# Gated cross-attention block: 128 instead of 256 moving columns in the second matmul of each score and PV product

## The chip, the cores and the metric

The kernel is written in Bass, with hand-placed semaphores, and runs on one core of one Trainium2 chip. A core has TensorE (matmul into PSUM), VectorE, ScalarE, GpSimd and SyncE, which here only issues DMAs. The metric is the device time of one execution in microseconds; the median of three executions is given, and one further execution was recorded by the profiler.

## The reference

A layer norm, cross-attention with 32 heads, a gated residual, a second layer norm, and a dense layer with LoRA adapters, for 32 batches of 64 tokens and 512 features:

```python
q = (hidden_q @ Wq).reshape(b, lq, h, dh)          # b=32, lq=64, h=32, dh=128
k = (hidden_kv @ Wk).reshape(b, lk, h, dh)
v = (hidden_kv @ Wv).reshape(b, lk, h, dh)
score = jnp.einsum('bqhd,bkhd->bhqk', q, k) * scale + position_bias
score = jnp.where(mask, score, neg_inf)
probs = jax.nn.softmax(score, axis=-1)
probs = jnp.where(mask, probs, 0)
ctx = jnp.einsum('bhqk,bkhd->bqhd', probs, v).reshape(b, lq, h * dh)
return ctx @ Wo
...
x = x + tanh(g_xattn[0]) * xattn(layernorm(x), ctx_4096, mask, position_bias, Wq, Wk, Wv, Wo)
x = x + tanh(g_ffn[0]) * ffn(layernorm(x), weight, bias, lora_A, lora_B, lora_start_indices)
```

The inputs are float32.

## The kernel before

**Precision.** Every matmul operand that matters is kept in two parts of type float32r (four bytes, of which TensorE uses a shortened mantissa): `hi` is the rounded value and `lo` the rest. A product of two such operands is made by `mm3` as three matmuls into the same PSUM bank: hi x hi, hi x lo, lo x hi, each with 512 moving columns in most places. The product lo x lo is left out there.

**Blocks and slots.** The 2048 rows are worked on in 4 blocks of 512 (8 batches). The main loop has one slot for each block and head, 128 in all, and each engine has its own instruction stream with a function `slot(n)`. TensorE's slot n is: the queries of head n (12 matmuls of `mm3`), the keys (12), one half of the value or output projection of a group of four heads (12), the two transposes of the probabilities of the slot before (line 437), the other half (12), then, in some slots, the transposes of the layer norm or the LoRA and dense work, then the scores of this slot and the PV product of the slot before. Order and waits are written out by hand; nothing schedules them.

**The score and PV block.** These two products are made differently. Four tiles m of 128 rows hold two batches each. For the scores, the stationary side is the queries of the tile, `qt_hi` or `qt_lo` (128 x 128), and the moving side is `kt[:, m, :, :, :]`, in which the hi part and the lo part of the keys lie side by side: 2 x 128 = 256 columns. `both` issues one matmul with the hi part of the stationary side and one with its lo part, both against all 256 columns, into `s_two[:, m, :, :]`, whose second index tells hi from lo of the moving side. So `s_two[:, m, 0, :]` holds (hi + lo) x hi, and `s_two[:, m, 1, :]` holds (hi + lo) x lo. VectorE adds the two halves as it scales them and adds the bias (line 746). The PV product is alike: stationary are the values `v` of tile t, hi or lo, moving is `pt[:, t, :, :]`, the transposed probabilities with hi and lo side by side, and the output is `pv_two[:, t, :, :]`, whose two halves are added by ScalarE and VectorE (lines 587 and 755). Each `both` has four tiles per product and slot, so a slot has 8 matmuls for the scores and 8 for PV.

**What waits for what around it.** The scores need `qt` and `kt` of this slot (written by ScalarE and VectorE). VectorE, GpSimd and ScalarE turn them into probabilities while TensorE makes the queries and keys of the next slot; GpSimd's scaling of `prob` (line 983) is what the transposes of line 437 wait for. ScalarE and VectorE copy the transposed probabilities into `pt` (lines 581 and 734), and PV waits for that. ScalarE takes PV's result out of PSUM (line 587).

In the names of the profile, `s_two<-kt,qt_lo` is a matmul into `s_two` with `kt` moving and `qt_lo` stationary; PE rows are matmuls and PEld rows are the loads of their stationary side, one for each.

Of the kernel before, what the change touches and what calls it, by code (L numbers as in the profile page):

```python
# [140 lines left out]
def flamingo_block(nc, x, ctxt, pair_bias, mask, wq, wk, wv, wo, g_xattn, g_ffn, wf, fbias, lora_a, lora_b,  # L141
                   lora_starts, lora_const, out):
    with ExitStack() as ctx:
# [131 lines left out]

        def both(pe, to, left, right):
            pe.matmul(to, left[0], right, start=True, stop=False)  # L277
            return pe.matmul(to, left[1], right, start=False, stop=True)  # L278

        block = ctx.enter_context(nc.Block())  # L280

# [92 lines left out]
        def _(pe):  # L374
# [65 lines left out]
            def scores(n):  # L440
                pe.wait_ge(q_lo, n + 1)
                pe.wait_ge(k_lo, n + 1)
                wait(pe, score_done, n)
                for m in range(PB):
                    mm = both(pe, s_two[:, m, :, :], [flat(q[:, m, :, :]) for q in qt], kt[:, m, :, :, :])
                mm.then_inc(s_ps, 1)

            def attention(n):
                g, h = divmod(n, G)
                pe.wait_ge(vo_free, NUMBER["v", g, PB - 1] + 1)  # L450
                pe.wait_ge(pt_lo, n + 1)
                for t in range(PB):
                    mm = both(pe, pv_two[:, t, :, :], parts(v, slice(None), h // 2 * (1 + g % 2), t, cols(h % 2, DH)), pt[:, t, :, :])
                mm.then_inc(pv_ps, 1)
# [608 lines left out]
```

## Time and profile before

| | us |
|---|---|
| median of 3 executions | 1824.71 (1824.16 to 1825.96) |
| the profiled execution | 1823.99 |
| span of its instructions | 1822.2 |
| matmuls | 8912, each with a weight load |
| of these on lines 277 and 278 | 4 x 512 |

The span is what the profile's views divide up; the execution's own time is 1.8 us longer. A busy time of TensorE is a sum of printed durations that overlap and whose ends are modelled; the distance from one start to the next is what a matmul takes from the engine in a dense run. Starts are printed in hundredths of a microsecond, so distances are read over several matmuls. The granted clock is 1.00 at full speed (2.4 GHz) and 0.5 at half (1.2 GHz).

### The profile page before, as it was taken

How to read it: one execution, taken by the hardware profiler on the slowest of the kernel's cores; microseconds unless marked ns; L12 is line 12 of the kernel's file. 1: busy time of each engine (PE TensorE's matmuls, PEld its weight loads, DVE VectorE, ACT ScalarE, POOL GpSimd, SP SyncE). 2: the span in 40 equal slices, each digit the busy share in tenths (PEclk: the TensorE clock that was granted, in tenths of full speed). 3: DMA queues.
4: the chain of work that ended last, by engine and by line, in shares of the span. 5: the costliest groups of instructions: out<-in, count | busy, mean ns of one | idle time of the engine just before them, and what ended most of it. 6: DMA issues, size and time to landing. Idle time of an engine off the chain costs nothing.

```text
span 1822.2 us, 25806 instructions
## 1 busy us (share of the span) xinstructions
PE 1774.6 (97%) x8912; PEld 1500.1 (82%) x8912; DVE 1165.9 (64%) x2257; ACT 808.7 (44%) x1608; POOL 923.0 (51%) x946
## 2 busy tenths in 40 slices
PE   5899999999999999999999999999999999999978
PEld 4788888888888888888888888888888888888866
DVE  4666667766677556766667656776667755666653
ACT  3444444444445434544445434444444543444430
POOL 3546455455555346554555534555555554545430
PEclk9999999999999999999999999999999999999987
DMA  3332333332332232323233223332323222232210
GB/s 119 93 114 82 104 99 110 99 94 86 98 100 87 93 110 92 112 81 105 81 104 93 88 93 110 98 105 91 95 83 101 90 82 98 81 99 83 91 35 24
DMA packets 93027, 168.76 MB, mean 93 GB/s; under 512 B 11313, under 2 KB 11441, under 8 KB 92898
## 3 DMA queue, kind: packets, MB, share of 16 engines
q1 hardware_dynamic: 91458, 165.52, 29.1%
q8 instruction: 72, 1.18, 0.3%
q10 hardware_dynamic: 1440, 1.59, 0.3%
q14 instruction: 57, 0.47, 0.1%
HBM read 162.88 MB, written 4.19 MB: 92 GB/s over the span
## 4 chain that ended last, share of the span: by engine, by line
PE 94%; DVE 3%; ACT 1%; issue 1%; DMA 0%; POOL 0%; SPq 0%; ACTq 0%; DVEq 0%
PE vo_bank L272 14%; PE vo_bank L274 14%; PE vo_bank L273 14%; PE q_bank L272 6%; PE q_bank L273 6%; PE q_bank L274 6%; PE k_bank L274 6%; PE k_bank L273 6%; PE k_bank L272 6%; PE pv_two L277 4%; PE pv_two L278 3%; PE s_two L278 3%; PE s_two L277 3%; PE pv_two L437 1%; PE vo_bank L461 1%; DVE wo_lo L689 1%
## 5 line engine op out<-in xcount | busy, mean ns | idle before, releaser
L973 POOL TENSOR_TENSOR score<-score,row_max 128x256 f32<-128x256 f32 x128 | 78.6, 614 | 679.3 <-DVE row_max L751 679.3
L929 POOL TENSOR_TENSOR ot_lo<-attn,ot_hi 128x512 fp32r<-128x512 f32 x128 | 165.6, 1294 | 112.9 <-ACT ot_hi L527 112.9
L272 PE MATMUL vo_bank<-wv_hi,ct_hi 128*128 128x512 f32 x512 | 205.6, 401 | 15.3 <-POOL wv_lo L929 15.3
L587 ACT ACTIVATE attn<-pv_two 128x512 f32<-128x512 f32 x128 | 76.7, 599 | 315.8 <-PE pv_two L278 315.8
L272 PE MATMUL vo_bank<-wo_hi,ot_hi 128*128 128x512 f32 x512 | 206.2, 403 | 3.5 <-POOL ot_lo L929 3.5
L272 PE MATMUL q_bank<-xt_hi,wq_hi 128*128 128x512 f32 x512 | 202.3, 395 | 1.4 <-DVE xt_lo L689 1.4
L273 PE MATMUL q_bank<-xt_lo,wq_hi 128*128 128x512 f32 x512 | 201.7, 394 | 0.0
L274 PE MATMUL vo_bank<-wo_hi,ot_lo 128*128 128x512 f32 x512 | 201.3, 393 | 0.0
L274 PE MATMUL vo_bank<-wv_hi,ct_lo 128*128 128x512 f32 x512 | 201.0, 392 | 0.0
L273 PE MATMUL vo_bank<-wo_lo,ot_hi 128*128 128x512 f32 x512 | 200.8, 392 | 0.0
L273 PE MATMUL vo_bank<-wv_lo,ct_hi 128*128 128x512 f32 x512 | 200.5, 392 | 0.0
L274 PE MATMUL q_bank<-xt_hi,wq_lo 128*128 128x512 f32 x512 | 200.2, 391 | 0.0
L274 PE MATMUL k_bank<-ct_hi,wk_lo 128*128 128x512 f32 x512 | 199.2, 389 | 0.0
L273 PE MATMUL k_bank<-ct_lo,wk_hi 128*128 128x512 f32 x512 | 199.2, 389 | 0.0
L272 PE MATMUL k_bank<-ct_hi,wk_hi 128*128 128x512 f32 x512 | 199.2, 389 | 0.0
L689 DVE TENSOR_TENSOR kt<-k_bank,kt 128x512 fp32r<-128x512 f32 x128 | 88.7, 693 | 146.5 <-ACT kt L527 146.5
L527 ACT ACTIVATE ot_hi<-attn 128x512 fp32r<-128x512 f32 x128 | 81.2, 634 | 219.2 <-DVE attn L755 219.2
L719 DVE TENSOR_TENSOR acc<-vo_bank,acc 128x512 f32<-128x512 f32 x128 | 88.4, 690 | 140.6 <-PE vo_bank L274 140.6
L929 POOL TENSOR_TENSOR wq_lo<-raw_q,wq_hi 128x512 fp32r<-128x512 f32 x128 | 166.2, 1299 | 21.7 <-ACT wq_hi L527 21.7
L929 POOL TENSOR_TENSOR wk_lo<-raw_k,wk_hi 128x512 fp32r<-128x512 f32 x128 | 175.1, 1368 | 2.1 <-ACT wk_hi L527 2.1
L929 POOL TENSOR_TENSOR wv_lo<-raw_vo,wv_hi 128x512 fp32r<-128x512 f32 x124 | 157.6, 1293 | 0.0
L689 DVE TENSOR_TENSOR wo_lo<-raw_vo,wo_hi 128x512 fp32r<-128x512 f32 x128 | 143.7, 1161 | 21.6 <-ACT wo_hi L527 21.5
(107 smaller groups left out, 4186.3 us busy)
## 6 DMA issues: line engine op xcount, KB each, us to landing
raw_vo<-in_wo SPq DMA_DIRECT2D x128, 256.0 KB, 3.3
raw_q<-in_wq SPq DMA_DIRECT2D x127, 256.0 KB, 2.6
raw_k<-in_wk SPq DMA_DIRECT2D x127, 256.0 KB, 2.8
raw_vo<-in_wv SPq DMA_DIRECT2D x124, 256.0 KB, 3.5
raw_bias<-in_pair_bias SPq DMA_DIRECT2D x64, 256.0 KB, 3.2
acc<-in_x SPq DMA_DIRECT2D x16, 256.0 KB, 5.4
out<-acc SPq DMA_DIRECT2D x16, 256.0 KB, 2.0
stage<-in_ctxt SPq DMA_DIRECT2D x14, 256.0 KB, 2.8
```

Of the source, the lines that this page charges most:

```text
L272: pe.matmul(to, left[0], right[0], start=first, stop=False)
L273: pe.matmul(to, left[0], right[1], start=False, stop=False)
L274: return pe.matmul(to, left[1], right[0], start=False, stop=last)
L277: pe.matmul(to, left[0], right, start=True, stop=False)
L278: return pe.matmul(to, left[1], right, start=False, stop=True)
L437: mm = pe.transpose(t_bank[:, cols(j, P)], flat(prob[:, cols(j, 2), :]), ident[:, :])
L527: act.activation(to, src, func).then_inc(done, 1)
L587: act.activation(by(attn, PB), pv_two[:, :, 1, :], ACT.Copy).then_inc(ot_b, 1)
L689: dve.tensor_tensor(to, src, f32(of), ALU.subtract).then_inc(done, 1)
L719: dve.tensor_tensor(acc[b % 2][:, t, :], bank_of(job)[:, :], acc[b % 2][:, t, :], ALU.add).then_inc(vo_free, 1)
L929: pool.tensor_tensor(to, src, f32(of), ALU.subtract).then_inc(done, 1)
L973: pool.tensor_tensor(score[:, :, :], score[:, :, :], row_max[:, :].unsqueeze(2).to_broadcast([P, PB, S]), ALU.subtract).then_inc(shift_don ...
```

## The change

```diff
         def both(pe, to, left, right):
             pe.matmul(to, left[0], right, start=True, stop=False)
-            return pe.matmul(to, left[1], right, start=False, stop=True)
+            return pe.matmul(to[:, 0, :], left[1], right[:, 0], start=False, stop=True)
```

`right` is `kt[:, m]` or `pt[:, t]`, whose second index is the part. With the change, the lo part of the stationary side meets only the 128 columns with the hi part of the moving side, and its matmul adds only to the first half of the output. The second half then holds hi x lo alone, and lo x lo is computed nowhere, as with `mm3`. The number, the order, the weight loads, the waits and the semaphore increments of TensorE's instructions stay as they are, and the instructions of all other engines and the DMAs are the same.

## Rows read from the trace of the kernel before

**Rows 1.** The page: busy time by engine, and the chain by engine.
```profile
PE 1774.6 (97%) x8912; PEld 1500.1 (82%) x8912; DVE 1165.9 (64%) x2257; ACT 808.7 (44%) x1608; POOL 923.0 (51%) x946
...
PE 94%; DVE 3%; ACT 1%; issue 1%; DMA 0%; POOL 0%; SPq 0%; ACTq 0%; DVEq 0%
```

**Rows 2.** Busy time from 60 to 1760 us; TensorE's waits there (total, times, longest).
```profile
core 0: us, PE busy (x) PEld busy (x) DVE busy (x) ACT busy (x) POOL busy (x), PEclk, DMA share, GB/s
60.00:1760.00 1700.00, 1695.76 (x8591) 1436.78 (x8591) 1113.10 (x2147) 779.22 (x1553) 893.47 (x907) 1.00 0.30 94
...
PE pv_two L277 <- DVE pt L734: 2.0, 4, 1.2
PE s_two L277 <- issue: 1.3, 1, 1.3
```

**Rows 3.** TensorE's waits over the whole run: total us, times, longest us.
```profile
PE vo_bank L272 <- POOL wv_lo L929: 15.3, 1, 15.3
...
PE pv_two L277 <- DVE pt L734: 5.1, 7, 1.9
```

**Rows 4.** TensorE's matmuls in order of time: start us, duration us, engine, line.
```profile
702.96 0.39 PE L272 MATMUL vo_bank<-wo_hi,ot_hi 128*128 128x512 f32 x1
...
703.64 0.28 PE L277 MATMUL s_two<-kt,qt_hi 128*128 128x256 f32 x1
703.76 0.28 PE L278 MATMUL s_two<-kt,qt_lo 128*128 128x256 f32 x1
...
704.60 0.28 PE L277 MATMUL pv_two<-pt,v_hi 128*128 128x256 f32 x1
...
705.44 0.28 PE L278 MATMUL pv_two<-pt,v_lo 128*128 128x256 f32 x1
705.56 0.40 PE L272 MATMUL q_bank<-xt_hi,wq_hi 128*128 128x512 f32 x1
```

**Rows 5.** Line 278 over the whole run: count, duration ns min/median/max.
```profile
L278 PE MATMUL s_two<-kt,qt_lo x512: 278/283/415, 42.7 to 1763.2; 128*128 128x256 f32 x171
...
L278 PE MATMUL pv_two<-pt,v_lo x512: 278/283/415, 56.1 to 1774.2; 128*128 128x256 f32 x171
```

**Rows 6.** TensorE's weight loads in the same score block, in order of time.
```profile
703.65 0.19 PEld L278 LDWEIGHTS s_two<-kt,qt_lo 128*128 128x128 f32 x1
703.76 0.19 PEld L277 LDWEIGHTS s_two<-kt,qt_hi 128*128 128x128 f32 x1
```

**Rows 7.** Weight loads at two places where TensorE had been idle.
```profile
65.98 0.19 PEld L277 LDWEIGHTS s_two<-kt,qt_hi 128*128 128x128 f32 x1 [1.51 <-issue]
66.09 0.19 PEld L278 LDWEIGHTS s_two<-kt,qt_lo 128*128 128x128 f32 x1
...
502.29 0.19 PEld L277 LDWEIGHTS pv_two<-pt,v_hi 128*128 128x128 f32 x1 [0.30 <-issue]
502.40 0.19 PEld L278 LDWEIGHTS pv_two<-pt,v_lo 128*128 128x128 f32 x1
```

**Rows 8.** Transposes (128 moving columns): eight in a row, durations, loads behind two.
```profile
30.87 1.03 PE L461 MATMUL vo_bank<-ident,xn 128*128 128x128 f32 x8
...
L461 PE MATMUL vo_bank<-ident,xn x128: 271/273/476, 30.9 to 1799.5; 128*128 128x128 f32 x128
...
700.79 0.19 PEld L272 LDWEIGHTS vo_bank<-wo_hi,ot_hi 128*128 128x128 f32 x1
700.89 0.19 PEld L273 LDWEIGHTS vo_bank<-wo_lo,ot_hi 128*128 128x128 f32 x1
```

**Rows 9.** Matmuls of the PV block at half clock, in order of time.
```profile
56.11 0.41 PE L278 MATMUL pv_two<-pt,v_lo 128*128 128x256 f32 x1
56.32 0.41 PE L277 MATMUL pv_two<-pt,v_hi 128*128 128x256 f32 x1
```

**Rows 10.** What other engines deliver to TensorE around the block, in order of time.
```profile
701.96 0.86 DVE L734 TENSOR_TENSOR pt<-pv_two,pt 64x256 fp32r<-64x256 f32 x2 [0.37 <-ACT pt L581]
...
710.02 0.62 POOL L983 TENSOR_TENSOR prob<-prob,row_scale 128x256 f32<-128x256 f32 x1
...
713.75 0.38 PE L437 MATMUL pv_two<-ident,prob 128*128 128x128 f32 x2
```

## The prediction

> **What bounds the kernel now.** I read the page first, from its busy shares to its chain. TensorE is busy for 97% of the span, and 94% of the chain that ended last is its own work; the next engine on the chain is VectorE with 3% [rows 1]. A busy share alone proves little for TensorE, whose matmul ends are modelled, so I asked for two more views. The table of stretches shows 1695.8 us of matmul in the 1700 us from 60 to 1760 at a granted clock of 1.00, and the list of waits of the same stretch has three entries, 3.8 us together (2.0, 1.3 and one of 0.5) [rows 2]. So between those points TensorE runs one matmul behind the other, and what one matmul costs is the distance from its start to the next start, not its printed duration: the 256-column matmuls have a duration of 283 ns but start every 120 ns. Outside that stretch TensorE waits more, 15.3 us for the first weights alone [rows 3], at the start and at the tail, which the change hardly touches.
>
> The starts give the price list. In the score and PV block of one slot sixteen 256-column matmuls start from 703.64 to 705.44, and the next one, of 512 columns, starts at 705.56: 1.92 us / 16 = 120 ns each. From the 512-column matmul at 702.96 to the first 256-column one at 703.64 lie three of 512 columns, 227 ns each [rows 4]. The difference of 256 columns is 107 ns, which is 256 / 2.4 GHz, and what is left over is 227 - 2 x 107 = 13 ns (120 - 107 = 13 ns too) for each matmul whatever its width. The granted clock is full there, so this is the upper level, 2.4 GHz.
>
> **The change, part by part.** It adds and removes no instruction and moves none: every `both` still issues two matmuls, each with its weight load, in the same order and with the same semaphores. The first (L277) is as it was. The second (L278) streams 128 columns in place of 256. There are 512 of these for the scores and 512 for PV [rows 5]; four of the first and eight of the second kind fall in the two short stretches of half clock, at the start and in the tail, so that 1012 run at full clock.
>
> By columns alone, the second matmul should go from 120 ns to 13 + 128 / 2.4 = 67 ns. [...] The views of the weight loads tell when the load runs: in this block the load of the next matmul starts 2 to 3 ns behind the start of the current one (load at 703.65 behind the matmul of 703.64, load at 703.76 with the matmul of 703.76) [rows 4, 6], so only one load is ahead, and the distance between two starts can't be shorter than one load. What a load takes is hidden in a block where starts are 120 ns apart. It shows where TensorE restarts from idle: there the first weights go in with nothing in flight, and the second load begins once the first is done. 65.98 to 66.09 and 502.29 to 502.40: 110 ns each as printed in hundredths [rows 7]; the printed duration of 0.19 us has a latency in it that overlaps. A sharper value comes from the four transposes of line 461 or the two of line 437, which have 128 moving columns: eight of them take 1.03 us in all, the last one 0.273 us of it, so they start every (1.03 - 0.273) / 7 = 108 ns. And behind two of them, the load for the 512-column matmul begins at 700.79 and the one after it at 700.89: 100 to 110 ns for one load of the float32r kind, beside a 128-column transpose [rows 8].
>
> So I take 108 ns for the distance from a 128-column second matmul to the next start: one load. The load for the second matmul itself is covered by the 256 columns of the first, as now. Per pair that is 120 + 108 = 228 ns in place of 240. The sum: 1012 x (120 - 108) = 12.1 us.
>
> At half clock the 256-column matmuls start every 210 ns [rows 9], which is 256 / 1.2 GHz, the lower level. If a load keeps its 108 ns there, the twelve matmuls win 12 x 0.1 = 1.2 us; if it is clocked like the columns it takes 216 ns and they win nothing. I take nothing, as no row shows a load at half clock that is shorter than 200 ns.
>
> Both bounds of the unknown: no row shows a float32r matmul with 128 moving columns. Upper end of the gain by the nearest rows: 108 ns for the second matmul, and the first one perhaps 113 ns in place of 120, as the first pair of the score block (703.64 to 703.76) is a little shorter than the others, if a stream that has ended early lets the pair close up; that is 760 x 7 ns = 5.3 us more, 17.4 us in all. Lower end: the second matmul at 120 ns still, no gain; at 113 ns, as that first pair, 7.1 us. I take the 108, because it is the only distance that rows show behind a matmul with 128 moving columns.
>
> What is late next? The score block ends 4 x 12 = 48 ns sooner and the PV block 96 ns sooner in each slot of some 13 us, and everything behind it comes forward with it. Two results of other engines have to be there. The transposed probabilities: VectorE has written them at 701.96 + 0.86 = 702.82, and the first PV matmul starts at 704.60 [rows 4], 1.8 us later. The scaled probabilities: GpSimd is done at 710.02 + 0.62 = 710.64, the transposes start at 713.75 [rows 10]. 48 ns doesn't use up such slack. Where TensorE waits for the transposed probabilities already (7 times in the run, 4 of them between 60 and 1760 [rows 2, 3]), the shorter score block ahead only lengthens the wait: 7 x 48 ns = 0.3 us given back. Net 12.1 - 0.3 = 11.8 us.
>
> Against the profiled execution: span 1822.2 - 11.8 = 1810.4 us, execution 1824.0 - 11.8 = 1812.2 us. Its time lies 0.7 us under the median of 1824.7, so the median forecast is 1824.7 - 11.8 = **1812.9 us**, 0.65% less.
>
> [...]
>
> **The rivals.**
>
> *No change.* The 13 ns above 107 belong to the exchange of weights and not to the stream, so that a start that waits for a load costs 107 + 13 = 120 ns again. For it: a load and 256 columns take the same 107 ns, so the block of before can't tell which of them carries the 13. Against it: the 108 ns behind the transposes and at the restarts [rows 7, 8]. It gives 1824.7 us. Chance 0.12.
>
> *The whole columns are won.* If the weights could go in two ahead, the second matmul would cost 67 ns and the gain is 1012 x 53 = 53.6 us, 1771 us. Against it: each load starts just behind the start of the matmul before it [rows 6]. [...] Chance 0.04.
>
> *Slower: narrow moving data run in several passes.* The transposes show that 128 columns of four-byte data can cost more than the line through 256 and 512 says: 108 ns where it says 67, about two times 53 ns [rows 8]. If a 128-column float32r matmul takes four times its columns, it costs 4 x 53 + 13 = 227 ns in place of 120, and the kernel loses 1012 x 107 = 108 us: 1933 us. Two passes would be hidden by the load; it decides from where the distance is over 120 ns. Against it: the transposes are plain float32, a transpose is another mode, and at 256 columns nothing of the kind shows. [...] Chance 0.11.
>
> *Slower: the clock.* The arrays stream fewer columns in the same blocks. A stretch of half clock of some 17 us, as in the tail, doubles what TensorE does in it and costs 8.5 us; two of them in mid-run turn the gain into a loss (1821 us with one, 1830 with two). Against it: the clock stays full from 60 to 1760 [rows 2], across blocks in which TensorE pauses for 1.2 and 1.3 us. Chance 0.03.
>
> **How the numbers follow.** The forecast has a chance of 0.70 and its own range is 1806.5 (both matmuls closer) to 1818 (113 ns). The range to hold 8 in 10 adds the case of no change (0.12) and so goes from 1806.5 to 1826, 1.3 us above the median for the scatter of the runs; it leaves out 0.18. A measurement of this kernel can tell about 0.2%, 3.6 us, from no change. Faster: 0.70 + 0.04 = 0.74. Same: 0.12. Slower: 0.11 + 0.03 = 0.14.
>
> **What would show it.** In the profile of the changed kernel the score and PV block should be 16 matmuls in about 8 x 0.228 = 1.82 us, with starts alternating between 120 and 108 ns; and the load that follows a second matmul should start with it. If the first is right and the span falls by less, waits of TensorE between 60 and 1760 should have grown beyond 4 us. Starts evenly 120 ns apart mean that the 13 ns is the exchange. A distance of over 200 ns behind L278 means passes. If the load of the next weights starts ahead of the current matmul, my one-load floor is wrong. If the time differs and the block doesn't, the prediction is wrong in a way that I don't see.

## The result and the profile after

The changed kernel takes 1819.8 us in the median of 15 executions (1816.9 to 1822.4), the kernel before 1824.3 us in 15 beside them (1822.6 to 1826.7). The ratio is 0.9975, 95% interval 0.9967 to 0.9982: faster by 0.25% or 4.5 us. The forecast was 11.8 us. The direction was right, but the gain is only 38% of the one forecast. The time lies inside the stated range of 1806.5 to 1826 only because that range was widened for the case of no change; it lies outside the forecast's own range, which ended at 1818.

The two profiled spans differ by just 1.7 us (1822.2 and 1820.5), so a difference of spans says little about where the gain went. What helps is that the program is periodic. From the first keys matmul (line 272) of slot 4 to the last line-272 one of slot 127 both kernels run the same order of instructions: 123 slots and nine more keys matmuls (2.0 us in each kernel). The rows below are the view of one tile, `k_bank`, from slot 4 on: engine and operation, count, duration in ns (min/median/max), first and last start in us. First the kernel before:

```profile
L272 PE MATMUL k_bank<-ct_hi,wk_hi x496: 389/389/389, 85.3 to 1760.0; 128*128 128x512 f32 x166
```

and the changed kernel:

```profile
L272 PE MATMUL k_bank<-ct_hi,wk_hi x496: 389/389/389, 89.2 to 1757.7; 128*128 128x512 f32 x166
```

This stretch took 1674.7 us before and 1668.5 us after: 6.2 us won, 50 ns a slot where 96 were forecast. And the changed kernel comes to slot 4 already 3.9 us late. These are two separate shortfalls. A third, small one is behind the last of these rows: 62.2 us to the end of the span before, 62.8 us after. Together: 6.2 - 3.9 - 0.6 = 1.7 us.

**The start.** The table of stretches shows a difference there. The columns are the stretch and its length, the busy time of each engine, the granted clock, the DMA share and GB/s. The kernel before and the changed one from 43.5 to 76.5 us:

```profile
43.50:76.50 33.00, 26.58 (x117) 21.64 (x117) 19.65 (x50) 13.55 (x28) 21.01 (x23) 0.90 0.31 95
```

```profile
43.50:76.50 33.00, 27.26 (x106) 22.06 (x107) 19.19 (x48) 11.30 (x25) 20.42 (x21) 0.74 0.34 95
```

The mean clock is 0.74 in place of 0.90, and TensorE gets 106 matmuls started where it had started 117. One more thing differs, and earlier. TensorE starts at 15.2 to 15.3 us in both, and its first matmuls of 512 columns stand 427 ns apart, at half clock. The first one that is shorter than 0.6 us, before and after:

```profile
19.25 0.42 PE L272 MATMUL vo_bank<-wv_hi,ct_hi 128*128 128x512 f32 x1
```

```profile
20.86 0.46 PE L273 MATMUL vo_bank<-wv_lo,ct_hi 128*128 128x512 f32 x1
```

Full clock comes 1.6 to 1.7 us later in this execution of the changed kernel, ahead of any matmul that the change touches. So not all of the 3.9 us need come from the change.

**The block.** TensorE's matmuls in order of time in the changed kernel, around a score and PV block (start us, duration us):

```profile
705.15 0.39 PE L274 MATMUL vo_bank<-wo_hi,ot_lo 128*128 128x512 f32 x1
705.38 0.28 PE L277 MATMUL s_two<-kt,qt_hi 128*128 128x256 f32 x1
705.49 0.22 PE L278 MATMUL s_two<-kt,qt_lo 128*128 128x128 f32 x1
705.55 0.34 PE L277 MATMUL s_two<-kt,qt_hi 128*128 128x256 f32 x1
705.72 0.22 PE L278 MATMUL s_two<-kt,qt_lo 128*128 128x128 f32 x1
...
707.11 0.22 PE L278 MATMUL pv_two<-pt,v_lo 128*128 128x128 f32 x1
707.17 0.45 PE L272 MATMUL q_bank<-xt_hi,wq_hi 128*128 128x512 f32 x1
707.45 0.39 PE L273 MATMUL q_bank<-xt_lo,wq_hi 128*128 128x512 f32 x1
```

These answer to [rows 4]. A first matmul (L277) now has a printed start only 60 ns behind that of the narrow one ahead of it, and a duration of 0.34 us in place of 0.28; from it to the next start it is 170 ns (705.55 to 705.72). Printed starts of matmuls don't come at an even pace here. Those of the weight loads come every 110 to 130 ns, so I read the distances from them, in the same block:

```profile
705.49 0.19 PEld L277 LDWEIGHTS s_two<-kt,qt_hi 128*128 128x128 f32 x1
705.60 0.19 PEld L278 LDWEIGHTS s_two<-kt,qt_lo 128*128 128x128 f32 x1
705.72 0.19 PEld L277 LDWEIGHTS s_two<-kt,qt_hi 128*128 128x128 f32 x1
...
706.88 0.19 PEld L277 LDWEIGHTS pv_two<-pt,v_hi 128*128 128x128 f32 x1
706.99 0.19 PEld L278 LDWEIGHTS pv_two<-pt,v_lo 128*128 128x128 f32 x1
707.11 0.19 PEld L272 LDWEIGHTS q_bank<-xt_hi,wq_hi 128*128 128x128 f32 x1
```

Before, two such loads stood 110 to 120 ns apart [rows 6]. Now they alternate: 110 ns as printed from the load behind a narrow matmul to the next, and 120 to 130 ns from there; in the trace's nanoseconds, as medians over many slots, 108 to 110 and 120 to 126 ns. From 705.49 to 707.11 lie seven pairs in 1.62 us, 231 ns a pair; before it was 240, and the forecast had 228. So the principle of the forecast (one load behind a narrow matmul, one 256-column stream behind a wide one) comes within 3 ns of each pair.

Then something is given back behind the block. From the first score matmul to the second matmul of the next queries it was 703.64 to 705.79 before and is 705.38 to 707.45 now. The printed hundredths give 2.15 and 2.07 us; the nanoseconds of the trace give 2.146 and 2.078 us, 68 ns ahead (73 ns at the third matmul of the queries). To the first keys matmul, eleven 512-column matmuls on, it was 4.66 us (708.30) and is 4.60 us. The row of the changed kernel:

```profile
709.98 0.39 PE L272 MATMUL k_bank<-ct_hi,wk_hi 128*128 128x512 f32 x1
```

60 ns are left. The 512-column matmuls behind the block don't start every 227 ns at once: before, the first five distances are mostly 228 to 236 ns, and in the changed kernel this lasts two matmuls longer.

I call the 75 of the 123 slots that take 13.07 us before plain slots; they have no layer norm, LoRA or dense work in them. Their median is the same 68 ns ahead behind the block, and 60 ns kept. The other 48 slots keep 39 ns in the mean, which brings the mean slot to 50 ns. TensorE waits a little more: the lists of waits from 90 to 1755 us have 1.3 us before and 2.3 us after. Before:

```profile
PE pv_two L277 <- DVE pt L734: 0.8, 3, 0.3
PE vo_bank L461 <- DVE v_lo L689: 0.5, 3, 0.2
```

After:

```profile
PE pv_two L277 <- DVE pt L734: 1.6, 6, 0.3
PE vo_bank L461 <- DVE v_lo L689: 0.7, 3, 0.2
```

### The profile page after: what moved, and what is told of

Same layout as the page of the kernel before. It is cut to its first block, busy times and chain, and to the rows that moved or that the text cites. A ratio compares the mean times of both kernels' runs of the same rounds, so it can differ in the third digit from the quotient of the medians.

```text
span 1820.5 us, 25806 instructions
## 1 busy us (share of the span) xinstructions
PE 1773.2 (97%) x8912; PEld 1495.9 (82%) x8912; DVE 1168.6 (64%) x2257; ACT 807.0 (44%) x1608; POOL 922.8 (51%) x946
## 4 chain that ended last, share of the span: by engine, by line
PE 93%; DVE 3%; ACT 1%; issue 1%; DMA 0%; POOL 0%; SPq 0%; ACTq 0%; DVEq 0%
PE vo_bank L272 13%; PE vo_bank L274 13%; PE vo_bank L273 13%; PE q_bank L272 7%; PE q_bank L274 6%; PE q_bank L273 6%; PE k_bank L274 6%; PE k_bank L272 6%; PE k_bank L273 6%; PE pv_two L277 5%; PE s_two L277 4%; PE pv_two L278 2%; PE s_two L278 2%; PE pv_two L437 1%; DVE wo_lo L689 1%
## 5 line engine op out<-in xcount | busy, mean ns | idle before, releaser
L272 PE MATMUL vo_bank<-wv_hi,ct_hi 128*128 128x512 f32 x512 | 205.9, 402 | 15.2 <-POOL wv_lo L929 15.2
L272 PE MATMUL q_bank<-xt_hi,wq_hi 128*128 128x512 f32 x512 | 211.2, 413 | 1.4 <-DVE xt_lo L689 1.4
L587 ACT ACTIVATE attn<-pv_two 128x512 f32<-128x512 f32 x128 | 76.5, 598 | 303.1 <-PE pv_two L278 303.1
```

What stands on the lines that cost most here:

```text
L272: pe.matmul(to, left[0], right[0], start=first, stop=False)
L587: act.activation(by(attn, PB), pv_two[:, :, 1, :], ACT.Copy).then_inc(ot_b, 1)
```

## Experiments

### The start: narrow late, narrow early, narrow from slot 2

The edit against the changed kernel, shortened:

```diff
-        def both(pe, to, left, right):
+        def both(pe, to, left, right, narrow):
             pe.matmul(to, left[0], right, start=True, stop=False)
-            return pe.matmul(to[:, 0, :], left[1], right[:, 0], start=False, stop=True)
+            if narrow:
+                return pe.matmul(to[:, 0, :], left[1], right[:, 0], start=False, stop=True)
+            return pe.matmul(to, left[1], right, start=False, stop=True)
...
+                    mm = both(..., n >= 4)      # late;  early: n < 4;  from slot 2: n >= 2
```

Expected of the late change:

> The second matmul is narrow (128 columns) from slot 4 on; in slots 0 to 3 it has 256 columns as before. In the profile of the changed kernel TensorE lost some 3.9 us on the kernel before by the third slot, most of it in added stretches of half clock between 45 and 76 us, and won 6.2 us from there to slot 127, 50 to 60 ns a slot. Theory A (the narrow matmuls of the first slots bring the half clock about): this kernel has the early slots of the kernel before and all of the later gain, so 1824.3 - 6 = 1818 us in every run, mean clock 0.989 or 0.990, runs within 1.5 us of each other. Theory B (the stretches come and go whatever the width): the runs scatter over 1817 to 1822 us as those of the changed kernel did, with clocks from 0.986 to 0.990, and those of the kernel before scatter by the same.

Measured: 1817.8 us (1816.2 to 1819.2, 5 executions), ratio 0.9963, interval 0.9950 to 0.9975. Clocks 0.989 or 0.990 in all five. The same row of `k_bank`:

```profile
L272 PE MATMUL k_bank<-ct_hi,wk_hi x496: 389/389/389, 85.0 to 1753.4; 128*128 128x512 f32 x166
```

1668.4 us for the stretch of 123 slots, as with the full change (1668.5), and slot 4 begins at 85.0, not 89.2. The clocks are those of theory A; the times lie 3 us apart, not within the 1.5 us that it expected. The clock from 43.5 to 76.5 us is that of before:

```profile
43.50:76.50 33.00, 26.83 (x123) 21.98 (x123) 20.15 (x50) 13.82 (x29) 21.76 (x23) 0.90 0.32 95
```

> Narrow second matmul in slots 0 to 3 only; everything from slot 4 on as before. Theory A (the width of the first slots brings the half clock): slower than the kernel before by about 4 us in most runs, mean clock about 0.986. Theory B: the same as the kernel before within 0.5 us in the median (4 slots x 60 ns = 0.2 us won), the scatter of both alike.

Measured: 1825.6 us (1823.3 to 1826.8, 11 executions), ratio 1.0005, interval 0.9996 to 1.0014: no difference that can be told. Theory A had about 4 us more. But the executions fall into two sorts: 7 of 11 have a mean clock of 0.987 or 0.988, with 1825.5 us or more, and 4 have 0.990, with 1823.3 to 1825.0. Of the 35 executions of the kernel before that stand beside these experiments, one is below 0.989. The profiled one is of the first sort:

```profile
L272 PE MATMUL k_bank<-ct_hi,wk_hi x496: 389/389/389, 89.1 to 1763.8; 128*128 128x512 f32 x166
```

It is 3.8 us late at slot 4 and still 3.8 us late at slot 127; the slots between take 1674.7 us, as before. Behind them it takes 60.5 us to the end, 1.7 us less than the kernel before. So the tail varies too, and a mean clock covers the start and the tail: it doesn't tell by itself where the half clock was.

> Narrow second matmul from slot 2 on, slots 0 and 1 wide. In the changed kernel's profile the first added stretch of half clock (some 2.4 us lost) lies about slot 1 and the second (2.7 us) at 69 to 76 us, slots 2 and 3. If the narrow blocks of slots 2 and 3 alone are enough, about half of the runs show a mean clock of 0.988 or less and take 1820 to 1822 us; if it takes the narrow blocks of slots 0 and 1, all runs are at 0.989 or 0.990 and 1816 to 1819 us.

Measured: 1817.0 us (1816.1 to 1822.4, 5 executions), ratio 0.9966, interval 0.9954 to 0.9979. One of the five has 0.987 and 1822.4 us, the other four have 0.989 or 0.990 and at most 1817.5 us. One in five is neither of the two outcomes that were expected (about half, or none).

What follows: neither theory as it was written. The 15 executions of the changed kernel are of two sorts too: 9 with a clock of 0.986 to 0.988 and 1819.5 to 1822.4 us, 6 with 0.989 or 0.990 and 1816.9 to 1818.0 us. With narrow matmuls in all of slots 0 to 3, 16 of 26 timed executions (changed kernel and early) have a mean clock below 0.989, against 1 of 35 of the kernel before. With slots 0 to 3 wide it is none of the 5 late ones and, in the runs further below, 1 of 6 and 0 of 5, and one profile (the last matmul wide) had the added half clock. So narrow first slots make it likely and don't force it, and wide ones don't quite exclude it. An execution with the lower clock takes 4.4 us longer in the changed kernel (medians 1821.9 and 1817.5 us) and 2.1 us longer in the early one (1826.1 and 1824.0).

A rival to the width of the first slots is left: the moment at which full clock first comes. In the three profiles with added half clock from 43.5 to 76.5 us (changed, early, and the last matmul wide) it first came at 21.0 to 21.3 us, in nine without it at 18.2 to 19.7. But in the two with 192 and 64 columns it came at 21.1 us as well, and no half clock was added; they came to slot 4 at 86.6 and 86.7 us, against 84.8 to 85.6 us for the nine. So a late first rise goes with some 1 to 1.5 of the 3.9 us by itself, and every added half clock that was profiled came with one. Whether it takes both, no run shows; what in the first blocks tips the clock wasn't isolated.

### Which half wins what

Same edit, `narrow` true for the scores alone or for PV alone, in all slots. Each of these two, and of the next three kernels, ran once.

> Narrow second matmul in the scores, 256 columns in PV as before. Of the gain per slot, 8 pairs x 12 ns = 96 ns forecast and 50 to 60 ns seen. Theory C (every 256-column matmul behind a narrow one starts its successor 2 to 4 ns later than before, and the first 512-column matmul of the queries 7 ns later): the scores win 4 x 9 = 36 ns a slot, none lost at the queries, since a wide matmul is last: 30 to 36 ns a slot. Theory D (a fixed price of some 40 ns a slot, paid elsewhere): 4 x 12 - 40 = about 8 ns a slot.

> Narrow second matmul in PV, 256 columns in the scores as before. Theory C: 4 x 9 = 36 ns won less 7 ns at the first 512-column matmul of the queries behind it: 22 to 30 ns a slot. Theory D: about 8 ns a slot, and the two halves together win more than their sum.

Measured, the `k_bank` rows of the scores alone and of PV alone:

```profile
L272 PE MATMUL k_bank<-ct_hi,wk_hi x496: 389/389/389, 85.0 to 1755.7; 128*128 128x512 f32 x166
```

```profile
L272 PE MATMUL k_bank<-ct_hi,wk_hi x496: 389/389/389, 85.6 to 1757.4; 128*128 128x512 f32 x166
```

1670.7 and 1671.8 us (the executions took 1820.4 and 1821.1 us): 33 and 24 ns a slot. Theory C has both, theory D (8 ns each) falls. In the mean slot the two sum to 57 ns, against 50 together; in the plain slots they keep 33 and 27 ns, which is the 60 of the change. In the scores alone, where the PV block behind is wide, the 33 ns won are all kept; PV alone is 35 ns ahead behind the block and keeps 27.

### Does the load bind: 192, 64, and 128 on both sides

From slot 4 on, the second matmul with 192 or 64 columns; and both matmuls with 128. With 64 columns half of lo x hi is left out, and with both at 128 all of hi x lo, so these two only serve to measure time. The edits against the changed kernel, shortened:

```diff
-                return pe.matmul(to[:, 0, :], left[1], right[:, 0], start=False, stop=True)
+                return pe.matmul(to[first 192 or 64 columns], left[1], right[the same], start=False, stop=True)
...
-            pe.matmul(to, left[0], right, start=True, stop=False)
+            pe.matmul(to[:, 0, :], left[0], right[:, 0], start=True, stop=False)     # both at 128
```

> From slot 4 on the second matmul has 192 moving columns, between the 128 of the change and the 256 of before (half of lo x lo is computed). Slots 0 to 3 as before, as in the kernel with the late change. Theory E (the distance to the next start is the longer of one weight load, 108 to 109 ns, and 13 ns + columns / 2.4): 13 + 80 = 93 ns is under the load, so 192 columns cost what 128 do, and a slot wins the same 50 to 60 ns. Theory F (cost falls with the columns, in proportion): half the gain, 25 to 30 ns a slot.

> From slot 4 on the second matmul has 64 moving columns; half of lo x hi is left out of the scores and of PV. Slots 0 to 3 as before. Theory E: the load of 108 to 109 ns binds as with 128 columns, 50 to 60 ns won a slot, nothing more. Theory F: 75 to 90 ns a slot.

> From slot 4 on the first matmul has 128 moving columns too; hi x lo is left out of the scores and of PV. Every distance of the block is then one load. Theory E: 16 x 109 = 1.74 us for the block in place of the 1.92 us of before and some 1.85 us of the change; per slot 16 x 11 = 176 ns won less 7 ns at the queries, 165 to 175 ns. If the loads themselves grow when they follow each other without a break (a load is 108 ns only when the array is otherwise idle for half the time), the distance is 115 to 120 ns and the gain 60 to 80 ns.

Measured, in this order:

```profile
L272 PE MATMUL k_bank<-ct_hi,wk_hi x496: 389/389/389, 86.6 to 1755.0; 128*128 128x512 f32 x166
```

```profile
L272 PE MATMUL k_bank<-ct_hi,wk_hi x496: 389/389/389, 86.7 to 1752.6; 128*128 128x512 f32 x166
```

```profile
L272 PE MATMUL k_bank<-ct_hi,wk_hi x496: 389/389/389, 85.5 to 1749.6; 128*128 128x512 f32 x166
```

192 columns: 1668.4 us (the execution took 1819.0 us), 51 ns a slot, just what 128 give. Theory E has it and theory F (half the gain) falls: between 128 and 192 columns the width of the second matmul is worth nothing. The distance behind the narrow matmul, read from the loads, is 108 to 110 ns with 192 columns as with 128, where 13 ns + columns / 2.4 gives 93 and 67 ns.

64 columns: 1665.9 us (the execution took 1815.6 us), 72 ns a slot, 80 in the plain slots. Theory E said 50 to 60; F said 75 to 90, but its proportion to the columns is out by the 192. The load behind the narrow matmul still takes its 108 to 110 ns; what shrank is the other distance of the pair, which its loads show:

```profile
701.97 0.19 PEld L277 LDWEIGHTS s_two<-kt,qt_hi 128*128 128x128 f32 x1
702.08 0.19 PEld L279 LDWEIGHTS s_two<-kt,qt_lo 128*128 128x128 f32 x1
702.19 0.19 PEld L277 LDWEIGHTS s_two<-kt,qt_hi 128*128 128x128 f32 x1
...
702.88 0.19 PEld L277 LDWEIGHTS pv_two<-pt,v_hi 128*128 128x128 f32 x1
```

Four pairs in 0.91 us are 228 ns each, which is the pair that was forecast for 128 columns. With half the columns again the 3 ns are gone. The block is 100 ns ahead at the second matmul of the queries, and 20 ns of that are given back. Why a wide matmul is slowed by 3 ns more behind 128 or 192 columns than behind 64 isn't explained by a floor of one load.

Both at 128: 1664.1 us (the execution took 1814.1 us), 86 ns a slot, where E said 165 to 175 and its alternative 60 to 80. The loads in the block:

```profile
700.03 0.19 PEld L282 LDWEIGHTS s_two<-kt,qt_lo 128*128 128x128 f32 x1
700.14 0.19 PEld L278 LDWEIGHTS s_two<-kt,qt_hi 128*128 128x128 f32 x1
700.25 0.19 PEld L282 LDWEIGHTS s_two<-kt,qt_lo 128*128 128x128 f32 x1
...
701.70 0.19 PEld L272 LDWEIGHTS q_bank<-xt_hi,wq_hi 128*128 128x128 f32 x1
701.81 0.19 PEld L273 LDWEIGHTS q_bank<-xt_lo,wq_hi 128*128 128x128 f32 x1
702.06 0.19 PEld L274 LDWEIGHTS q_bank<-xt_hi,wq_lo 128*128 128x128 f32 x1
```

From 700.03 to 701.70 lie 15 distances, 111 ns each. That is the cost of a float32r matmul of 128 columns whose neighbours are no wider. It is 3 ns over the 108 that the forecast took for a load, and 3 ns is also what a load's start lies behind the start of the matmul beside it. At the load for the third matmul of the queries (702.06, which goes with the start of their second) the block stands at 2.03 us against 2.15 before, 120 ns ahead; 93 ns are kept in the plain slots. The give-back is 27 ns here, 8 ns in the changed kernel counted from the same matmul (13 from its peak).

### The order: two wide, two narrow

From slot 4 on, with nothing left out that the change computes. The two tiles of a pair, m and m + 2, lie 512 float32 columns apart in PSUM. The edit for the scores, shortened; PV has the same:

```diff
+                    for m in range(2):
+                        for j in (m, m + 2):
+                            pe.matmul(s_two[:, j, :, :], hi of tile j, kt[:, j, :, :, :], start=True, stop=False)
+                        for j in (m, m + 2):
+                            mm = pe.matmul(s_two[:, j, 0, :], lo of tile j, kt[:, j, 0, :, :], start=False, stop=True)
```

> From slot 4 on the same matmuls as in the change, in another order: two first (256 columns) of two tiles that lie in different PSUM banks, then their two second ones (128 columns). Nothing is left out that the change computes. Theory G (a matmul of 256 or 512 columns that starts right behind its own load, with no earlier stream still running, takes some 3 to 7 ns more): it is now 4 of the 8 first matmuls in place of 8 that start so, and the slot wins 3 x 4 = 12 ns more than the late change does, 62 to 75 ns in the plain slots in place of 60. Rival: the 3 ns belong to every 256-column matmul whose next one is narrow or to the load of the second part; then the order changes nothing.

> The paired order again, timed. In the look at it its plain slots were 66 ns shorter than before (late change: 60), and it gave 1817.5 us against 1824.5. Theory A again (narrow matmuls in slots 0 to 3 bring the half clock there): wide in those slots, it should show mean clocks of 0.989 or 0.990 in every run, as the late change did. Forecast: 1817 us, 0.7 us under the late change, which its scatter of 3 us may hide.

Measured: 1817.9 us (1816.2 to 1819.0, 6 executions), ratio 0.9965, interval 0.9953 to 0.9977; an execution ahead of these, profiled too, took 1817.5 us. The slots:

```profile
L272 PE MATMUL k_bank<-ct_hi,wk_hi x496: 389/389/389, 85.6 to 1753.4; 128*128 128x512 f32 x166
```

1667.8 us, 56 ns a slot against 51 of the late change (1667.7 us in the other profile). The plain slots keep 7 ns more, 67 in place of 60; theory G expected 2 to 15 more and its rival nothing. But the 7 ns are not where theory G put them. From the first score matmul to the second matmul of the queries:

```profile
701.48 0.40 PE L452 MATMUL s_two<-kt,qt_hi 128*128 128x256 f32 x2
...
703.56 0.40 PE L273 MATMUL q_bank<-xt_lo,wq_hi 128*128 128x512 f32 x1
```

That is 2.08 us, and 2.08 us in the late change (701.12 to 703.20). The order wins nothing in the block (67 and 68 ns ahead in the plain slots); what differs is that the queries behind it give nothing back. So theory G isn't borne out, though its number came true. In time the kernel can't be told from the late change. All clocks were 0.989 but one, of 0.988. Counted as above, that one is low; its time, 1816.2 us, is the shortest of the six, and no profile tells where its half clock lay.

### The last matmul wide

As the late change, with `n >= 4 and t < 3` for PV, so that tile 3 has its 256 columns back. It ran once.

> As the late change, but the last tile of PV has its second matmul wide (256 columns): 7 narrow ones a slot. Seen so far: with all 8 narrow, the block is 68 to 73 ns ahead of before at the second 512-column matmul of the queries behind it, and 12 to 13 ns of that are given back over the next six; with only the scores narrow, the block is 33 ns ahead and nothing is given back. Theory H (the give-back comes when the last matmul ahead of the queries is narrow): 57 ns ahead at the end of the block and 57 ns kept, 3 ns short of the full change. Theory I (it grows with the number of narrow ones): some 57 - 11 = 46 ns kept.

Measured:

```profile
L272 PE MATMUL k_bank<-ct_hi,wk_hi x496: 389/389/389, 89.5 to 1757.0; 128*128 128x512 f32 x166
```

1667.5 us for the slots: 59 ns a slot with seven narrow matmuls, more than with eight (51). In the plain slots the 60 ns won at the end of the block are all kept. Theory H has this, theory I falls. In the plain slots the last narrow matmul of the change is worth nothing; the 8 ns in the mean slot come from the other 48 slots (56 ns in place of 39). Theory H doesn't fit the paired order, though, which ends on a narrow matmul and gives nothing back. This profile is also the one that began 4.2 us late though its first four slots are wide; it took 1819.5 us.

### Both together

Late, paired, and the last matmul wide.

> What the runs so far say a faster version should be, all outputs of the change kept: slots 0 to 3 wide as before; from slot 4 on the paired order in the scores and in PV, and the very last matmul of PV (low part of tile 3) wide again, since it was worth nothing when narrow. If both effects add up, the plain slots are 66 to 70 ns shorter than before and the mean slot 60 to 66 ns (late change 51, paired 56, last one wide 58), so 1824.5 - 8 = 1816.5 us against 1817.8 for the late change. If they are the same effect seen twice, the plain slots stay at 60 to 66 ns and the time at 1817 to 1818 us.

Measured: 1818.0 us (1816.6 to 1818.3, 5 executions), ratio 0.9966, interval 0.9952 to 0.9980.

```profile
L272 PE MATMUL k_bank<-ct_hi,wk_hi x496: 389/389/389, 85.3 to 1755.4; 128*128 128x512 f32 x166
```

1670.1 us: 37 ns a slot (33 in the plain ones), less than either part alone. For the slots this is outside both expectations; the time alone would have fitted the second. The block itself is 59 ns ahead at its end, as in the kernel with the last one wide, but the queries give back 26 ns although the matmul ahead of them is wide. So theory H isn't the rule.

The kernels side by side: how many ns the plain slots are ahead of before at the second matmul of the queries, what they keep a slot later, and what the mean slot keeps.

| kernel | ahead behind the block | kept, plain slots | kept, mean slot |
|---|---|---|---|
| scores alone | 33 | 33 | 33 |
| PV alone | 35 | 27 | 24 |
| the change, late, 192 columns | 68 | 60 | 50 to 51 |
| last matmul wide | 60 | 60 | 59 |
| paired | 67 | 67 | 56 |
| paired, last wide | 59 | 33 | 37 |
| 64 columns | 100 | 80 | 72 |
| both at 128 | 120 | 93 | 86 |

## Why the prediction was right and wrong

**Right: what bounds the kernel.** TensorE's starts set the time, and no other engine took over (93% of the chain that ended last, after 94%). What the block wins the slot wins, but for what the next matmuls give back and 1 us of added waits.

**Right: the load, not the columns.** The forecast put the second matmul at one load and against 67 ns by columns. The loads at 110 ns, and 192 columns that cost as much as 128, bear it out. The rival that wins all the columns would have given 1771 us and is out. So is the slower one by four passes, with its 227 ns: no run shows its factor of four, and a narrow float32r matmul has 111 ns with both at 128. Two passes, which the load would hide at 128 columns, would be 160 + 13 = 173 ns at 192 columns, and those cost no more than 128. The rival of no change is out too: the starts aren't 120 ns apart.

What the runs show is the distance: in none of the profiles here do the loads of two float32r matmuls, one behind the other, start less than 108 ns apart. That a matmul is held until its own weights are in, no run shows. The load for the first score matmul behind a pause starts at 65.98 us in the kernel before [rows 7], and the matmul's printed start is 30 ns later:

```profile
66.01 0.36 PE L277 MATMUL s_two<-kt,qt_hi 128*128 128x256 f32 x1 [1.30 <-issue]
```

**Wrong: the term 1012 x (120 - 108) = 12.1 us.** It treated the pair as 120 + 108. Measured it is 231 ns, not 228, so 9 ns a pair are won and not 12. The 108 came from transposes and restarts [rows 7, 8], and no row had a narrow float32r matmul. With both matmuls at 128 columns each distance is 111 ns. The text had the 2 to 3 ns by which a load starts behind its matmul [rows 6] and didn't add them; adding them gives the 111 and the 231. That this is their cause isn't shown: in the changed kernel the loads are 108 to 110 ns apart behind the narrow matmul and the excess is behind the wide one, and with 64 columns the pair has 228 ns. The block wins 68 ns a slot and not 96, which over 123 slots is 3.4 us of the shortfall.

**Wrong: that everything behind the block comes forward with it.** Nothing was charged to the 512-column matmuls behind the block. They give back 8 ns a plain slot in the changed kernel (13 from the peak), some 1 us in all. The trace of before had a sign of it: the first matmuls of the queries stood 228 to 236 ns apart and not 227, and I read the price of 227 from the end of a run of them.

**Wrong: that no wait grows.** 0.3 us was the forecast; the waits from 90 to 1755 us grew by 1.0 us.

These three take the stretch from the forecast 984 x 12 ns = 11.8 us to about the 6.2 measured (11.8 - 3.4 - 1.0 - 1.0 = 6.4).

**Wrong: the clock as a rival of little weight.** It was priced at 8.5 us a stretch and placed in mid-run with a chance of 0.03. It came at the start, where the list of waits already had TensorE pausing, and I had called that part hardly touched. 9 of 15 executions have the lower clock and take 4.4 us more. That is what parts the median of all, 1819.8 us, from that of the other six, 1817.5 us. Of the 7.3 us between the forecast gain and the measured one, then, 2.3 go with the clock, and the other 5.0 are about what the loop fell short by. The late change, at 1817.8 us, had no such execution among its five, and the same gain in the loop.

**Two slips in the working.** The lower end of the range, 1806.5 us, doesn't follow from 17.4 us of gain: 1824.7 - 17.4 = 1807.3. And the 108 ns a load were read from transposes, but not every load of theirs takes that: those for the plain float32 transposes start 56 to 65 ns apart 16 times in the trace of before, as in these rows, where the loads had been idle. Those of float32r don't come below 108. Neither changes the forecast.

```profile
743.61 0.14 PEld L461 LDWEIGHTS vo_bank<-ident,xn 128*128 128x128 f32 x1 [0.56 <-issue]
743.66 0.14 PEld L461 LDWEIGHTS vo_bank<-ident,xn 128*128 128x128 f32 x1
```

Left open: where the 3 ns of each pair come from, what fixes how much the queries give back (nothing in three kernels, 8, 20 and 26 to 27 ns in the others, with no order in it by what stands last), and why the half clock at the start comes in one execution and not the next.

The late, the paired and the combined version all lie at 1817.8 to 1818.0 us, 0.34 to 0.37% under the kernel before and by 2 us under the median of the change. They can't be ranked among each other by time. The late change is the simplest.

## What to carry to other kernels

In the score and PV block of this kernel, where each float32r matmul has a new stationary side, a pair of them took, within 3 ns, what you get by giving each the longer of 111 ns (the distance measured with both at 128) and 13 ns + columns / 2.4 (read at 256 and 512 columns): 231 ns with 192 or 128 columns in the second, 228 ns with 64. So narrowing the second from 256 columns to 192 or 128 won about 9 ns, and from 192 to 128 nothing. Price a change of a few nanoseconds on the whole period of the loop, from one landmark to the same one a slot later, because the matmuls behind it can give back a part (up to 27 ns a slot here); one row with first and last start over a hundred slots shows 1 ns a slot (two profiles of the paired kernel had 1667.7 and 1667.8 us). And look at the start of a kernel, where TensorE pauses, apart from the loop: here narrow first blocks went with more half clock (a low mean clock in 16 of 26 executions against 1 of 35).

## What the runs showed of the hardware that was not expected

- The printed start of a 256-column matmul behind a narrow one is 60 ns behind it, with 0.34 us printed in place of 0.28, while the loads there start 110 ns apart; so the distances here are read from the loads.
- The first 512-column matmuls behind a block of shorter ones, or behind two transposes, start mostly 228 to 236 ns apart before they settle at 227: five distances in the kernel before, seven in the changed one, more in the kernels that give back 20 ns or more.
- The gains kept by the plain slots were 27, 33, 60, 67, 80 and 93 ns in the kernels tried, whatever the block had won: all within 1 ns of multiples of 6.67 ns. What makes them so wasn't tested.
- This program's first rise to full clock came at 18.2 to 21.3 us with the same first matmuls, and with narrow matmuls in the first four slots TensorE often got more half clock: granted 0.74 in place of 0.90 from 43.5 to 76.5 us in the profile, and a low mean clock in 16 of 26 executions against 1 of 35 of the kernel before.
- The loads of plain float32 transposes started as little as 56 ns apart, those of float32r never under 108.
